# A graph network kernel in which tile 22's weighted products and additions are placed ahead of tile 23's aggregation

## The reference

```
for layer in (L0, L1, L2, L3):
    h = relu(layernorm(x));  x = x + layer(h, edges)

L0: t1 = h@W1;  msg = (t1[src] + (h[src]*h[dst])@W2) / (sqrt(outdeg[src])*sqrt(outdeg[dst]))
    e = where(in_count > 0, t1 + segment_sum(msg, dst), 0) + b
    e = leaky_relu(e);  e = e / max(norm(e), 1e-12)
L1: weighted graph convolution with self loops: norm = dinv[row]*w*dinv[col],
    segment_sum((h@W)[col]*norm, row), then a two-layer MLP
L2: h@W0.T + b0 + segment_sum((h@W1.T + b1)[src], dst), batch norm, relu
L3: attention over the edges (4 heads of 64), softmax per dst, elu
```

## Time and profile before

| | us |
|---|---|
| median of 3 runs | 2202.52 (2201.77 to 2205.61) |
| the profiled execution | 2199.41 |
| its span in the profile | 2195.9 |
| mean granted TensorE clock | 0.893 of full |
| busy in the span: PE / PE weight loads / DVE / ACT / POOL | 1857.6 / 1148.2 / 1346.7 / 485.3 / 1085.4 |

### The profile page before, as it was taken

How to read it: one execution, slowest core, us unless ns; L and a number is a source line. 1 busy time by engine, 2 the same in 40 slices (tenths; PEclk the granted TensorE clock), 3 DMA queues, 4 the chain that set the end, 5 groups by cost and what they waited for, 6 DMA issues and landing times. The chain is left out here.

```text
span 2195.9 us, 23174 instructions
## 1 busy us (share of the span) xinstructions
PE 1857.6 (85%) x7239; PEld 1148.2 (52%) x7239; DVE 1346.7 (61%) x2027; ACT 485.3 (22%) x639; POOL 1085.4 (49%) x1563
## 2 busy tenths in 40 slices
PE   5499858779999999646655599999989999999996
PEld 1178622247777776534433365778863444434443
DVE  7977779855554444223322235656578787878877
ACT  1000110025555554323322252400160000000000
POOL 1888788888888888888888800000005000000000
PEclk9755579889999999878877799999989999999999
DMA  7788850016666666324433353196525555656544
GB/s 284 322 337 333 326 203 9 9 59 242 240 240 240 240 240 240 137 104 159 142 120 123 122 220 99 43 314 215 175 68 157 150 158 168 191 162 177 164 139 128
DMA packets 339275, 394.93 MB, mean 180 GB/s; under 512 B 114448, under 2 KB 320634, under 8 KB 326267
## 3 DMA queue, kind: packets, MB, share of 16 engines
q1 hardware_dynamic: 220297, 306.93, 40.0%
q10 hardware_dynamic: 93110, 86.22, 11.8%
q0 software_dynamic: 25792, 0.88, 1.0%
HBM read 221.43 MB, written 172.51 MB: 179 GB/s over the span
## 5 line engine op out<-in xcount | busy, mean ns | idle before, releaser
L377 POOL DMA_INDIRECT table<-valT,idxT x806 | 810.1, 1005 | 163.6 <-issue 162.6
L2028 PE MATMUL psum<-wgt,big 128*65 128x384 f32 (+4 forms) x1600 | 531.0, 493 | 9.8 <-DVE wgt L1979 9.6
L1979 DVE SCALAR_TENSOR_TENSOR wgt<-ratio,l3q,fcj 128x768 f32<-128x768 f32 (+4 forms) x442 | 408.5, 949 | 92.7 <-PE psum L2028 82.3
L2028 PEld LDWEIGHTS psum<-wgt,big 128*65 128x65 f32 x1600 | 219.0, 138 | 312.6 <-issue 282.9
L789 PE MATMUL psum<-hx,region 128*128 128x257 f32 x1250 | 301.7, 390 | 5.0 <-DVEq L577 5.0
L789 PE MATMUL psum<-region,g 128*128 128x512 f32 (+1 forms) x672 | 270.1, 547 | 1.0 <-DVE big L592 1.0
L592 DVE TENSOR_TENSOR big<-big,psum 128x512 f32<-128x512 f32 (+1 forms) x325 | 209.7, 665 | 86.8 <-PE psum L789 86.4
L375 POOL MEMSET rest<- 128x256 f32 x722 | 237.0, 328 | 48.2 <-DVEq L490 47.7
L789 PEld LDWEIGHTS psum<-hx,region 128*128 128x128 f32 x1250 | 235.4, 197 | 36.4 <-DVEq L577 5.4
L857 PE MATMUL psum<-ident,tk 128*128 128x128 f32 x625 | 105.9, 307 | 168.9 <-DMA tk<-table 168.3
L857 PEld LDWEIGHTS psum<-ident,tk 128*128 128x128 f32 x625 | 99.0, 207 | 176.4 <-DMA tk<-table 170.4
(11 more groups left out here) (220 smaller groups left out, 1607.8 us busy)
## 6 DMA issues: line engine op xcount, KB each, us to landing
table<-tk SPq DMA_DIRECT2D x25, 3200.0 KB
fcj<-counts SPq DMA_DIRECT2D x125, 384.0 KB, 3.5
tk<-table SPq DMA_DIRECT2D x25, 1664.0 KB
counts<-region ACTq DMA_DIRECT2D x25, 1600.0 KB, 9.7
tk<-table SPq DMA_DIRECT2D x25, 1536.0 KB
fcj<-counts SPq DMA_DIRECT2D x46, 448.0 KB, 3.7
counts_t<-region ACTq DMA_DIRECT2D x25, 800.0 KB
counts_b<-region ACTq DMA_DIRECT2D x25, 800.0 KB
```

Of the source, the lines that this page charges most:

```text
L377: eng.indirect_dma_start(out=table, out_offset=bass.IndirectOffsetOnAxis(idxT[:, c:c + 1], 0), in_=valT[:, c, :], in_offset=None).then_inc ...
L1979: eng.scalar_tensor_tensor(out=wgt[:, n % NW, u, 0:w], in0=rb[:, 2 * i + u, t0 * P:t0 * P + w], scalar=qs[:, k, 2 * i + u:2 * i + u + 1], ...
L2028: last = eng.matmul(acc[p % 2][u][0:FW, b, 0:hi - lo], ftx[:, k, 2 * i + u, :], wgt[:, n % NW, u, lo:hi], start=k == 0, stop=k == NT - 1, ...
```

## The change

`overlapped` passes `ahead=True` to the step with `cur` = 23 and `prev` = 22. The loop and the two calls after it keep their order. In that one step:

- TensorE makes all 13 chunks of `gathered` of tile 22, then the aggregation and transposes of tile 23 (now the function `sums`), then the transposes of groups 0 to 2 of tile 24 (now `next_turned`), then `turn_ab`, then `dense`.
- ScalarE copies the weights of tile 22 into `wt` before `normal(22)` and no longer between the takes of groups 4 and 5.
- VectorE makes the 13 `lift`s and `own` of tile 22 (one addition to `xs`, L601) directly behind `diag`, before `q` and `ab` of tile 23.

The number of instructions on each engine and their operands stay the same.

```diff
--- before.py
+++ after.py
@@ -76,7 +76,7 @@
     with eng.Fori(0, m - 1) as i:
         step((2 * i + 1, 1, i), (2 * i, 0))
         step((2 * i + 2, 0, i + 1), (2 * i + 1, 1))
-    step((NT - 2, 1, m - 1), (NT - 3, 0))
+    step((NT - 2, 1, m - 1), (NT - 3, 0), ahead=True)
     step((NT - 1, 0, m), (NT - 2, 1), last=True)
     step(None, (NT - 1, 0))
 
@@ -579,7 +579,7 @@
             ch2 = Chain(eng, sem("dve2"))
             begun = ch.n
 
-            def step(cur, prev, last=False):
+            def step(cur, prev, last=False, ahead=False):
                 row = lambda t, k: t[:, bass.ds(k, 1), :].rearrange("p a d -> p (a d)")
 
                 def lift(n):
@@ -608,6 +608,10 @@
                 if prev and cur:
                     eng.wait_ge(sem("wt"), prev[0] + 3)
                     itself(row(wt, prev[0]))
+                if ahead:
+                    for n in range(13):
+                        lift(n)
+                    own()
                 if cur:
                     k, s, r = cur
                     ch.n, ch.rounds = begun, 13 * k
@@ -623,10 +627,10 @@
                     eng.tensor_tensor(ab[:, 1, :], q[:, :], hk[:, :], ALU.mult).then_inc(sem("ab"), 1)
                 if last:
                     itself(tk[:, s, k, :, 1])
-                if prev:
+                if prev and not ahead:
                     for n in range(5 if last else 13):
                         lift(n)
-                if prev and not last:
+                if prev and not last and not ahead:
                     own()
                 if cur:
                     eng.wait_ge(sem("e"), k + 1)
@@ -741,16 +745,19 @@
                 eng.activation(to[:, :], xs[:, bass.ds(k, 1), :].rearrange("p a d -> p (a d)"), ACT.Relu,
                                bias=ln1[:, 3:4], scale=ln1[:, 2:3]).then_inc(sem("g1"), 1)
 
-            def step(cur, prev, last=False):
+            def step(cur, prev, last=False, ahead=False):
                 if not cur:
                     return
                 k, s, r = cur
                 one = lambda t: t[:, bass.ds(k, 1)]
+                if ahead:
+                    eng.wait_ge(sem("ag"), 13 * prev[0] + 1)
+                    eng.activation(wt, tk[:, prev[1], :, :, 1], ACT.Copy).then_inc(sem("wt"), 1)
                 if prev:
                     normal(prev[0], g1)
                 take(k, 3)
                 take(k, 4)
-                if prev:
+                if prev and not ahead:
                     eng.wait_ge(sem("ag"), 13 * prev[0] + 1)
                     eng.activation(wt, tk[:, prev[1], :, :, 1], ACT.Copy).then_inc(sem("wt"), 1)
                 take(k, 5)
@@ -857,8 +864,8 @@
                     last = eng.transpose(pC[:, g % 3, o:o + P], tk[:, s, j, :, 0], ident[:, :])
                 last.then_inc(sem("tc"), 1)
 
-            def step(cur, prev, last=False):
-                if cur:
+            def step(cur, prev, last=False, ahead=False):
+                def sums():
                     k, s, r = cur
                     eng.wait_ge(sem("ab"), k + 1)
                     for g in range(7):
@@ -873,6 +880,15 @@
                             turn(k, s, g + 3)
                     mul.then_inc(sem("q"), 1)
 
+                def next_turned():
+                    eng.wait_ge(sem(f"tk{1 - s}0"), 16 * (r + s) + 16)
+                    for g in range(3):
+                        turn(k + 1, 1 - s, g)
+                if cur:
+                    k, s, r = cur
+                    if not ahead:
+                        sums()
+
                 def gathered(chunks):
                     j, z = prev
                     of, g = (wt, g1) if cur else (tk[:, 0, :, :, 1], hk)
@@ -899,6 +915,13 @@
                 if prev:
                     eng.wait_ge(sem("g1"), prev[0] + 1)
                     eng.wait_ge(sem("diag"), prev[0] + 1)
+                if ahead:
+                    gathered(range(13))
+                    sums()
+                    next_turned()
+                    turn_ab()
+                    dense()
+                    return
                 if not cur:
                     gathered(range(13))
                     return
@@ -911,9 +934,7 @@
                 if prev:
                     gathered(range(5, 13))
                 if not last:
-                    eng.wait_ge(sem(f"tk{1 - s}0"), 16 * (r + s) + 16)
-                    for g in range(3):
-                        turn(k + 1, 1 - s, g)
+                    next_turned()
             eng.sem_inc(sem("ag"), 1)
             eng.wait_ge(sem("cols"), QB)
             eng.wait_ge(sem("tk00"), 16)
```

## The result

| | us |
|---|---|
| before, median of 5 runs | 2204.95 (2201.77 to 2207.99) |
| changed, median of 5 runs | 2214.84 (2214.35 to 2215.92) |
| ratio changed / before | 1.0048, 95% interval 1.0033 to 1.0063 |
| predicted | 2214.1, range 2209 to 2219 |
| the profiled execution of the changed kernel | 2214.35, span 2211.8 |

The account below looks back on a forecast made before the run. Tile 23's load bounds the kernel until 1267 us, TensorE's list from then on. Terms sum to 10.0 us by position and 11.6 with the clock, taking the median from 2202.52 to 2214.1, range 2209 to 2219.

Parts of the forecast that it names:

- The idle time stays empty: TensorE's 25.99 us wait for tile 23's load, ending step 22, stays unfilled because products move only within step 23.
- Wait for `g1`: Step 23, before tile 22's products: TensorE idles about 7.6 us while ScalarE makes the weights copy, then `normal(22)`.
- Aggregation, transposes of tile 24, `turn_ab`: Step 23 after the products: aggregation 12.45 us (1.1 won back), transposes 1.43, then `ab` 0.25 late for `turn_ab`.
- `dense` and the first take: End of step 23: TensorE waits 0.7 us for `abT` before `dense`, then 1.9 for tile 24's first take.
- The clock: Tile 22's products start at half clock after TensorE's idle gap, costing 1.6 us, bounds 0 and 1.7.
- 3.4 us at half speed: Assumed length of the slow start of tile 22's products, costing at most 1.7 us.
- The second fall of the clock: Rival: gaps between `turn_ab` and tile 24's aggregation slow TensorE again, another 1.7 us, sum 13.3; chance 0.15.
- Step 24: Order kept but ScalarE has no lead; stall set at nothing. Rival with ScalarE late: +15 us, chance 0.10.
- the thin cover: Step 24: take 3 done at 1314.5, wanted by TensorE at 1315.1, leaving 0.6 us.
- An earlier load of tile 24: Step 23: the load's last pair comes about 5.5 us earlier, gaining nothing because TensorE did not wait for it.
- The 0.35 for rows that no longer overlap: Term in the sum: about 0.35 us added for rows that no longer overlap.
- the case in which the clock never falls: Rival: TensorE's clock stays warm across the idle gap, so +10.0 us, 2212.5; chance 0.20.

Follow-up runs that it names:

- the control: Kernel before with steps 21 and 22 written out behind the loop, no order changed: ratio 0.9984 on the 2309.02 us chip, later 2203.82 us, ratio 1.0004.
- ScalarE's part alone: Kernel before with only ScalarE's copy of tile 22's weights moved ahead of `normal(22)`, TensorE and VectorE unchanged: ratio 0.9992.
- the first and third experiments: Changed kernel with the weights copy after `normal(22)`: ratio 1.0070; changed kernel with copies `ct` and `cb` moved earlier on ScalarE: ratio 1.0020.
- the filled kernels: Kernel before with steps 21, 22 written out and tile 22's products ending step 22: ratios 1.0065, 0.9972, 0.9974; variants moving `ct`, `cb`: 1.0105, 0.9981, 0.9950.
- the first two filled runs: Kernel before with tile 22's products put at the end of step 22: ratio 1.0065 without a load wait, then 2198.10 us, ratio 0.9972, with one.
- The four experiments of the first group: Changed kernel with `normal(22)` before copy: 1.0070; `ct`, `cb` earlier: 1.0020; 26 zero products in TensorE's wait: 1.0046. Kernel before with ScalarE's edit only: 0.9992.

## Why the prediction was right

Point by point, in the prediction's own steps:

- **The idle time stays empty.** Right. 25.97 us before the transposes, and the kernels with the products at the end of step 22 show that the place, not the idea, was the fault: 6 us gained in B, not 12 lost.
- **Wait for `g1`.** 7.54 us named, 7.6 expected. The sum of copy and `normal` was shown by the swapped order (7.91).
- **Aggregation, transposes of tile 24, `turn_ab`.** Within 0.1 us: the aggregation took 1303.81 - 1291.41 = 12.40 for 12.45, and `ab` was 0.20 us late for 0.25.
- **`dense` and the first take.** 0.69 and 2.00 for 0.7 and 1.9, and the second shown to be `cb` by moving the copies (2.17 less). There is luck in the 1.9. I took 0.34 us for `cb`'s DMA issue from tile 24's step and gave no reason; in tile 23's step, the one that changes, it had taken 4.75. At that length the takes would have come 4.4 us later, and the forecast would have been near 2218.5. The issue was long in the two kernels in which it came some 10 us behind SyncE's issue of tile 24's load (before, and the control with 4.91), and took 0.34 us at 16 us behind it (ScalarE's part alone) and at 34 (the changed kernel). That the load is the reason is likely by this, and not shown.
- **The clock.** The one term that was off. Taken at 1.6, bound 1.7; it is 2.0 in the changed kernel. The step that failed is the bound, "3.4 us at half speed". Nine traces have these 28 products behind a gap of 6.8 to 7.9 us. They took 12.53 to 14.02 us, 1.5 to 3.0 more than the 11.01 at full clock. In these traces the clock rose 3.1 to 6.1 us after the products began, not 3.4 at most. I had also put the clock as risen at 1270.4 and fallen again. It had not risen in the changed kernel, but that is not why the bound failed: where it did rise and fall again, in the first and third experiments, the cost was 2.9 and 3.0, and behind a gap entered at full clock (the filled kernels) 1.5 to 2.8.
- **The second fall of the clock.** Not in the changed kernel: 1.00 from 1306 to 1311 and after. Of the six traces with the same gap of 2.00 us, two show it (the first two filled runs: 3.34 and 2.79 us for the first piece of the aggregation, 1.98 without), and four do not. So its absence here was chance, as far as the runs tell. The Trainium skill ("TensorE: Matmul & The Clock Gate", section "HAM oscillation — how this bites in real kernels") tells of a kernel in which each burst behind a wait for a DMA starts slow. The traces agree for the gaps of 6.8 to 7.9 us. The waits of that kernel are longer than the 0.7 and 1.9 us for which I charged a second fall, so that charge did not follow from what the Trainium skill says.
- **Step 24.** Its own length, B - A, is 40.82 against 40.79: the thin cover held.
- **An earlier load of tile 24** gained TensorE no time, as shown by ScalarE's part alone; whether it kept `cb`'s DMA issue short is the open point above.

In sum 12.2 us in the profile for 11.6 predicted. Counted from start to start, TensorE's rows give 7.75 for the wait, 2.09 for the products, -1.15 for the aggregation, 0.36 and 0.90 up to `dense`, and 2.28 up to tile 24's aggregation: 10.1 without the products' slow start, for 10.0 predicted. The 0.35 for rows that no longer overlap had no row behind it.

That the median came out within 0.7 us of 2214.1 is partly luck. The median of before rose by 2.4 with two more runs, and the medians lie 9.9 apart for a forecast difference of 11.6. By the medians alone, the case in which the clock never falls (2212.5) could not be told from mine; the windows tell them apart.

## What to carry to other kernels

An idle stretch belongs to the instruction that waits at its end. Before moving work in front of something to fill it, look at which list entry holds each engine during the stretch (here tile 23's transposes and takes, both in the step before) and whether the moved work's own inputs can be made on engines that are not held there. A block of work that is whole loses its use as cover: the products in three pieces had hidden `abT`, `cb` and the takes, and the aggregation in front of them had hidden `g1`. Every one of them came out as a wait.

## What the runs showed that I had not expected

- The kernel before ran at 2203 to 2205 us in four groups of runs and at 2309 in one. In that one, engines waited for remote events, up to 14 us each, in the steps that run beside GpSimd's indirect DMAs, and hardly at all once these had ended, at 1261 to 1268. The four experiments of the first group show such waits too, up to 9.2 us, in steps before 1100 us; there TensorE had caught up long before tile 23, so the idle time was the same. The first and the last group carry the same chip number, and the last has no such wait, so the chip alone may not be the reason. What delays the events stays open.
- An order that fills a wait for a load gains 0.26 to 0.28% where the wait exists and loses 0.65% where it does not.
- A DMA issue on ScalarE's queue took 0.34 to 0.40 us in most rows, but 3.21 once directly behind another large one, and that of `counts_b` up to 7.5 us in others, with no issue directly before it. Such a row is hidden as long as ScalarE has a wait behind it, and a change of order can bring it out.
- The cost of a slow start of TensorE for the same 28 products was 1.5 to 3.0 us in nine traces of nearly the same code.
- Behind B there is a chance of its own. The first row of eight matmuls of the next stage, behind gaps of 1.48 and 0.78 us, took 3.70 us in the kernel before and the changed one, and 5.30 in the control of the last group, which changes no order: there the granted clock had fallen to 0.50 in the gap. Totals of single executions differ by 1.6 us for this alone.
